# Mixture-of-experts rows written to DRAM by token and rank with indirect stores, and read back with sixteen plain loads

## The reference, cut to what matters

```python
scores = softmax(x @ w_router.T)                    # 1024 tokens x 64 experts
topw, topi = top_k(scores, 6)
combine[token, topi] = topw
routed = sum over experts e of combine[:, e:e+1] * (silu(x @ wg[e]) * (x @ wv[e])) @ wo[e]
shared = (silu(x @ swg) * (x @ swv)) @ swo
x = layernorm(x + routed + shared)                  # x: 1024 x 256, wg/wv: 64 x 256 x 176
```

## Time and profile before

| | us |
|---|---|
| median of 3 runs | 1000.24 |
| lowest, highest | 993.20, 1004.77 |
| the profiled execution | 987.55 |
| its span, first to last instruction | 985.7 |
| outside the span | 1.85 |
| mean granted TensorE clock | 0.961 |
| busy: PE, DVE, ACT, POOL | 870.2, 720.6, 510.4, 407.1 |

### The profile page before, as it was taken

How to read it: one execution, slowest core, us unless ns; L and a number is a source line. 1 busy time by engine, 2 the same in 40 slices (tenths; PEclk the granted TensorE clock), 3 DMA queues, 4 the chain that set the end, 5 groups by cost and what they waited for, 6 DMA issues and landing times.

```text
span 985.7 us, 15418 instructions
## 1 busy us (share of the span) xinstructions
PE 870.2 (88%) x5267; PEld 568.3 (58%) x5271; DVE 720.6 (73%) x1377; ACT 510.4 (52%) x1022; POOL 407.1 (41%) x338
## 2 busy tenths in 40 slices
PE   7999999999999999988889999999546867899886
PEld 3466666666565666656666777677423654343443
DVE  5667786959696867768774556665467798998797
ACT  3563554545544444445444334455522457898485
POOL 0203448494848577534214333333377312221013
PEclk9999999999999999989999999999866998999998
DMA  5451212112131221100926999999633000000001
GB/s 189 153 196 27 65 49 86 70 65 77 58 102 53 81 75 65 44 1 1 238 94 216 298 311 310 313 312 303 179 96 98 26 1 3 5 8 6 1 6 38
DMA packets 54743, 106.46 MB, mean 108 GB/s; under 512 B 8909, under 2 KB 26645, under 8 KB 54165
## 3 DMA queue, kind: packets, MB, share of 16 engines
q1 hardware_dynamic: 48917, 89.88, 29.6%
q0 software_dynamic: 5760, 15.74, 6.0%
HBM read 88.45 MB, written 17.14 MB: 107 GB/s over the span
## 4 chain that ended last, share of the span: by engine, by line
PE 54%; DVE 19%; DMA 10%; issue 5%; ACT 5%; SPq 3%; POOL 3%; DVEq 0%; ACTq 0%; POOLq 0%
PE ps L777 10%; PE ps L715 6%; DMA w_dn<-in_w_dn 5%; PE ps L873 5%; PE ps L725 4%; DVE row_max L2696 3%; PE ps L948 3%; DMA y_dram<-y_out 3%; PE ps L1280 3%; POOL key_part L1507 2%; DVE state L2119 2%; PE ps L795 2%; PE ps L960 2%; DMA key_part<-y_dram,slot_idx 2%; PE ps L1266 2%
## 5 line engine op out<-in xcount | busy, mean ns | idle before, releaser
L1479 POOL DMA_INDIRECT xg<-x_dram,tok_of x68 | 65.1, 958 | 131.8 <-PE ps L1006 94.2
L777 PE MATMUL ps<-w_vg,xT 128*128 128x512 f32 x256 | 116.8, 597 | 1.2 <-DVE th L2162 1.2
L1429 POOL TENSOR_TENSOR state<-state,rows_bc 128x1024 f32<-128x1024 f32 x22 | 53.8, 2446 | 95.5 <-DVE state L2119 41.9
L715 PE MATMUL ps<-xT,w_qks 128*128 128x512 f32 x192 | 86.5, 596 | 5.2 <-ACT qT L1585 5.2
L948 PE MATMUL ps<-w_gv,xgT 128*128 128x352 f32 (+1 forms) x272 | 87.4, 464 | 2.5 <-DMA w_dn<-in_w_dn 2.4
L2696 DVE TENSOR_REDUCE row_max<-ps 128x4 f32<-128x1024 f32 x64 | 74.3, 1217 | 7.1 <-PE ps L1245 6.3
L2130 DVE TENSOR_TENSOR aT<-ps,tri 128x768 f32<-128x768 f32 x64 | 59.7, 954 | 27.0 <-PE ps L725 26.9
L1585 ACT ACTIVATE probT<-ps 128x512 f32<-128x512 f32 x128 | 69.5, 594 | 10.1 <-PE ps L1266 9.6
L777 PEld LDWEIGHTS ps<-w_vg,xT 128*128 128x128 f32 x256 | 45.8, 190 | 48.8 <-issue 43.1
L960 PE MATMUL ps<-w_dn,hidT 88*128 88x256 f32 (+1 forms) x272 | 70.0, 379 | 0.0
L948 PEld LDWEIGHTS ps<-w_gv,xgT 128*128 128x128 f32 x272 | 48.9, 190 | 27.0 <-issue 5.2
(11 more groups left out here) (327 smaller groups left out, 2066.6 us busy)
## 6 DMA issues: line engine op xcount, KB each, us to landing
w_gv<-in_w_gv SPq DMA_DIRECT2D x68, 352.0 KB, 8.2
rows_bc<-x_dbl_dram SPq DMA_DIRECT2D x32, 512.0 KB, 3.8
w_dn<-in_w_dn SPq DMA_DIRECT2D x68, 192.0 KB, 9.6
y_dram<-y_out SPq DMA_DIRECT2D x68, 128.0 KB, 7.5
y_dram<-blank SPq DMA_DIRECT2D x4, 1408.0 KB, 13.2
w_vg<-in_wvg SPq DMA_DIRECT2D x8, 512.0 KB, 4.9
w_qks<-in_wqks SPq DMA_DIRECT2D x8, 384.0 KB, 3.1
w_o<-in_wo SPq DMA_DIRECT2D x8, 256.0 KB, 2.7
```

What stands on the lines that cost most here:

```text
L715: last = mm(bank(PJ + n % 2), w_qks[:, k, part * P:(part + 1) * P], xT[:, k, half * 512:(half + 1) * 512], start=(k == 0), stop=(k == KD - 1))
L777: last = mm(bank(PJ + t % 2), xT[:, k, t * P:(t + 1) * P], w_vg[:, k, :], start=(k == 0), stop=(k == KD - 1))
L1429: G.tensor_tensor(state_of(m), state_of(m), c_row[:, n % 2], ALU.mult).then_inc(read_out, 1)
L1479: G.indirect_dma_start(xg[:, j, :], None, x_dram, bass.IndirectOffsetOnAxis(ap=col, axis=0)).then_inc(gathered[j], 16)
```

## The change

Every row of an expert's result goes to the row of `y_dram` that belongs to its token and rank, 8 * token + rank with ranks 1 to 6 (two rows in eight stay unused). A row that belongs to no token goes to a spare row behind them. So POOL's indirect DMAs are now stores in the loop, two columns behind the gathers, and the combining reads three ranks of 128 tokens at once with a plain load on SP's queue.

- **Routing:** `scale_hot` is six ACT instructions per tile, each with the code 8 * token + rank (`tok_code`), and PE waits for each. DVE makes `tok_of` from the codes in three instructions behind one copy, drops `slot_idx`, and makes `row_of` with two more behind `groups`. Two more constants are loaded (`tok_code`, `spare`), ahead of `sh_gv` and the expert weights in SP's order.
- **Loop:** SP issues no stores. POOL, in pass i, issues for each j gather (i + 1, j), then waits for `down_copied` and issues scatter (i - 1, j). `y_out` has two halves in the fixed groups, so DVE's copy waits for the store of two groups ago. The dynamic group uses half 0 alone, waits for the scatter of the group before, and its POOL pass starts after the gathers *and* the scatters before it have landed; it copies two sets of column numbers. The last four scatters follow behind it with a third set.
- **Combining:** 16 loads of 384 KB on SP (3 KB from each of 128 token rows), four buffers, behind `f_in` and `f_out` and behind all `y_stored`.
- **Gone:** `blank`, its memset and its four stores.

```diff
-        yg = key_part[:].rearrange("p a b c -> p (a b c)").bitcast(F32).rearrange("p (n d) -> p n d", d=D)
+        yg = key_part[:].rearrange("p a b c -> p (a b c)").bitcast(F32).rearrange("p (n d) -> p n d", d=CHUNK * D)
...
-        y_out = sb("y_out", [P, NJ, D])
+        y_out = sb("y_out", [P, 2, NJ, D])
...
-            for n in range(4):
-                dst = y_dram[(E + NJ) * P + n * free:(E + NJ) * P + (n + 1) * free, :]
-                sp.dma_start(dst.rearrange("(n p) d -> p n d", p=P),
-                             blank[:].unsqueeze(1).to_broadcast([P, free // P, D])).then_inc(y_blank, 16)
...
-            def store_y(i, j):
-                sp.wait_ge(down_copied, at(i, NJ, j + 1) + TILES)
-                sp.sem_inc(load_due, 1)
-                sp.dma_start(y_dram[bass.ds(i * (NJ * P) + j * P, P), :], y_out[:, j, :]).then_inc(y_stored[j], 16)
...
             sp.wait_ge(stacked, 6)
             for dst, src in ((f_in, "f_in"), (f_out[:], "f_out")):
                 sp.dma_start(dst, a[src]).then_inc(layer_loaded, 16)
+            for j in range(NJ):
+                sp.wait_ge(y_stored[j], at(used, 16, 0))
+                sp.sem_inc(load_due, 1)
+            by_token = y_dram[0:RANKS * TOK, :].rearrange("(q e) d -> q (e d)", e=RANKS)
+            for c in range(2 * TILES):
+                if c >= 4:
+                    sp.wait_ge(combined, B + CHUNK * (c - 3))
+                first = (1 + CHUNK * (c % 2)) * D
+                sp.dma_start(yg[:, c % 4, :], by_token[c // 2 * P:(c // 2 + 1) * P, first:first + CHUNK * D]
+                             ).then_inc(back[c % 4], 16)
...
             for i in range(FIXED):
                 for j in range(NJ):
                     pool.wait_ge(xg_turned, NJ * i + j + 1)
                     gather(j, tok_of[:, NJ * (i + 1) + j:NJ * (i + 1) + j + 1])
+                    if i == 1 and j == 0:
+                        pool.wait_ge(rows_placed, 1)
+                    if i:
+                        pool.wait_ge(down_copied, NJ * (i - 1) + j + 1 + TILES)
+                        scatter(i % 2, j, row_of[:, NJ * (i - 1) + j:NJ * (i - 1) + j + 1])
             used = used_groups(pool)
             with pool.Fori(FIXED, used) as i:
                 for j in range(NJ):
                     pool.wait_ge(gathered[j], at(i, 16, 16))
-                pool.sem_inc(gather_due, 1)
+                    pool.sem_inc(gather_due, 1)
+                    pool.wait_ge(y_stored[j], at(i, 16, -16))
+                    pool.sem_inc(gather_due, 1)
                 G.tensor_copy(tok_cur[:], tok_of[:, bass.ds(i * NJ + NJ, NJ)]).then_inc(tok_picked, 1)
...
+                G.tensor_copy(row_cur[:], row_of[:, bass.ds(i * NJ - NJ, NJ)]).then_inc(row_picked, 1)
...
                     gather(j, tok_cur[:, j:j + 1])
-
+                    pool.wait_ge(down_copied, at(i, NJ, j + 1 - NJ + TILES))
+                    pool.sem_inc(gather_due, 1)
+                    scatter(0, j, row_cur[:, j:j + 1])
+            G.tensor_copy(row_last[:], row_of[:, bass.ds(used * NJ - NJ, NJ)]).then_inc(last_picked, 1)
...
             for j in range(NJ):
-                pool.wait_ge(y_stored[j], at(used, 16, 0))
-            pool.sem_inc(gather_due, 1)
-            pool.wait_ge(stacked, 6)
-            for n in range(TILES * TOPK):
-                if n >= 8:
-                    pool.wait_ge(combined, B + n - 7)
-                G.indirect_dma_start(yg[:, n % 8, :], None, y_dram,
-                                     bass.IndirectOffsetOnAxis(ap=slot_idx[:, n // TOPK, n % TOPK:n % TOPK + 1], axis=0)
-                                     ).then_inc(back[n % 8], 16)
+                pool.wait_ge(down_copied, at(used, NJ, j + 1 - NJ + TILES))
+                pool.sem_inc(gather_due, 1)
+                scatter(0, j, row_last[:, j:j + 1])
...
-                f(blk_hot[:, t % 2], blk_hot[:, t % 2], ACT.Copy, scale=tok_id[:, t:t + 1]).then_inc(hot_scaled, 1)
+                for k in range(TOPK):
+                    f(blk_hot[:, t % 2, k, :], blk_hot[:, t % 2, k, :], ACT.Copy, scale=tok_code[:, t, k:k + 1]
+                      ).then_inc(hot_scaled, 1)
...
-            V.tensor_copy(tok_of[:], ps[:, Y + 1, 0:COLS]).then_inc(route_vec, 1)
+            V.tensor_copy(code_f, ps[:, Y + 1, 0:COLS])
+            then(V.tensor_scalar(tok_f, ps[:, Y + 1, 0:COLS], -0.5 * (TOPK + 1), 1.0 / RANKS, ALU.add, ALU.mult))
+            then(V.tensor_scalar(tok_f, tok_f, ROUND, None, ALU.add))
+            V.tensor_scalar(tok_of[:], tok_f, -ROUND, None, ALU.add).then_inc(route_vec, 1)
...
-                    if not first:
+                    if half is None:
                         dve.wait_ge(y_stored[j], at(i, 16, 0))
-                    V.tensor_scalar(y_out[:, j, :], ps[:, 2 * j + 1, 256:512], 0.5, None, ALU.mult).then_inc(down_copied, 1)
+                    elif i > 1:
+                        dve.wait_ge(y_stored[j], at(i, 16, -16))
+                    V.tensor_scalar(y_out[:, half or 0, j, :], ps[:, 2 * j + 1, 256:512], 0.5, None, ALU.mult).then_inc(down_copied, 1)
```

More of the change, by code:

```diff
@@ L489, in build @@
         down_copied = sem("down_copied")
-        y_blank = sem("y_blank")
-        back = [sem(f"back{j}") for j in range(8)]
+        rows_placed = sem("rows_placed")
+        row_picked = sem("row_picked")
+        last_picked = sem("last_picked")
+        back = [sem(f"back{j}") for j in range(4)]
         combined = sem("combined")
@@ L1406, in _ @@
             nc.gpsimd.memset(x_pad[:, :, :, 0:DC - 1], 0.0).then_inc(pool_set, 1)
-            nc.gpsimd.memset(blank[:], 0.0).then_inc(pool_set, 1)
             G = nc.gpsimd
@@ L2457, in stack, with group @@
                     last.then_inc(stacked, 1)
-            def group(i, first=False, side=None):
+            def group(i, half=None, side=None):
                 for j in range(NJ):
```

73 lines of the change are left out of this document (44 added, 29 removed).

## The result

In the timing that followed the prediction the changed kernel took 1040.65 us (median of 4 runs, 1039.31 to 1043.03), the kernel before 997.98 us beside it. The ratio is 1.0425, with a 95% interval of 1.0357 to 1.0493. Forecast were 993.5 us, a range of 981 to 1010, and no measurable difference as the likeliest of the three outcomes.

The account below looks back on a forecast made before the run. Combining was POOL-bound by issuing gathers; the loop had DMA share 1.04 and PE busy 135.14 of 140 us. Terms -11.0 + 0.3 + 1.5 + 2.5 = -6.7 us, taken from 1000.24 us, gave 993.5 us, range 981 to 1010 us.

Parts of the forecast that it names:

- no measurable difference: Whole kernel: within about 1%, 10 us, of before, chance 0.46; faster 0.34, slower 0.20.
- The loop: Expert loop: stores move to POOL, eight DMAs a group, period 10.5 us instead of 10.42; +1.5 us.
- rival A: Loop becomes bound by POOL and its gathers: +19.5 or +27 us, time 1011.5 or about 1019 us; chance 0.24.
- the signs that the prediction named: Changed profile: additions from about 711 to 762 us, groups of 10.4 to 10.6 us, chunks landing in 3 to 4 us.
- Combining stage: Combining: sixteen SP loads replace 48 POOL gathers; 15.9 us of gaps go, 4.9 return as PE waits; -11.0 us.
- Routing: Routing: six ACT instructions replace one, more DVE instructions and two constants are added; +0.3 us, bounds -1.5 and +1.5.
- The formula: Loop: a group's period is 9.96 us plus half of what the gathers' landing exceeds 5.47 us.
- POOL's floor: Loop: POOL's eight DMA issues at 1.255 us each bound a group at 10.04 us.
- The gain to be set against it: Loop: the 0.68 us a group for which PE waits because of late `y_out` copies would go.
- rival B: Loop gets faster too, -4 us, and combining gains 14 instead of 11: -15 us, 985 us; chance 0.28.
- The end of the loop: Dynamic pass and last scatters: later gathers and waits for scatters make the first addition start 2.5 us later; +2.5 us.
- A rule that the forecast weighed: Loop scatters: write receipt is longest to HBM, so scatters land later than gathers and rival A is likelier; no size given.

Follow-up runs that it names:

- e11: The changed kernel, not altered, timed again beside the kernel before: 984.53 us against 987.13, ratio 0.9976.
- four later timings: The unaltered changed kernel timed on four other occasions, on chips with four different numbers: 984.53, 987.21, 986.13 and 984.78 us.
- e1: The kernel before with only the sixteen combining loads of the changed one in place of the 48 gathers: 976.94 us against 987.91, ratio 0.9887.
- e16: The changed kernel, not altered, timed again beside the kernel before: 984.78 us against 989.91, ratio 0.9977.
- e3: The changed kernel with plain stores issued by POOL, in slot order, in place of the scatters: 977.85 us, a single run.
- e4: The kernel before with a second gather behind each gather of the sixteen fixed groups, into a tile nothing reads: 1044.62 us.
- e8: The kernel before with second gathers as in e4, but two buffers for them: 1019.11 us, a single run.
- e13: The changed kernel, not altered, timed again beside the kernel before: 987.21 us against 987.73, ratio 0.9992.
- e2: The changed kernel with the scatters' row numbers in slot order, so each writes 128 neighbouring rows: 981.1 us, a single run.
- e15: The changed kernel, not altered, timed again beside the kernel before: 986.13 us against 989.18, ratio 0.9972.
- Experiment 12: The changed kernel with POOL issuing each pass's four gathers first, then its four scatters: 981.58 us, ratio to before 0.9939.
- e14: The gathers-first kernel with the wait for older stores and the row-number copy moved behind the last pass's gathers: 981.52 us against 989.18, ratio 0.9909.
- first ten experiments: Variants of the changed kernel (row numbers, layout, kind of store) and of the kernel before (new combining loads, second gathers): 976.94 to 1044.62 us.

## Why the prediction was wrong, step by step

**Against the first timing** it was wrong in its range and direction. The step that failed is "The loop": +1.5 us (with rival A's +27 at most), where +62.7 came up to the last `y_out` copy, 55 of them in the fourteen passes. Rival A was slower for another reason than its own: it asked for a POOL-bound group, with a scatter issue of 1.5 us or more or gathers that land after 7.4 us. There POOL idled 45.0 us waiting for PE, and a scatter took 1.01 us; landings can't be read in that trace. What the runs show in its place: a group of 14.9 us in which ACT takes PE's results 5.4 us after their matmuls start, against 1.5 in e11, and this in that trace alone. Its cause stays open. No row of the trace before could show it.

**Against the four later timings** the forecast of no measurable difference holds, and the gain was put too high: 0.7% forecast, 0.1 to 0.3% measured. The range of 981 to 1010 us holds all four too, but the kernel before also ran 10 to 13 us faster there than the 1000.24 that it was built on, so only the ratios count. Most of the signs that the prediction named are there in e11: groups of 10.6 us, DVE waiting for PE's projection, PE waiting for late gathers, and a scatter under 1.1 us (1.01 in the mean). The steps that failed in size are the fourteen passes, and the first pass of the loop, which had no term:

- *Combining stage, -11.0 us.* Right: 50.0 to 52.6 us in place of 61.6, so -9.0 to -11.6 (e1, with the old loop: -10.4). The mechanism too: a load landed in 3.5 us (3.1 assumed), no addition but the first waited for one in e11 (in e16 the fourth too, 1.45 us), and 4.9 us were to come back as waits for PE. In e11's waits of 700 to 770 us they are 5.1, and 6.3 to 6.7 in the other three:

```profile
DVE lk L2555 <- PE ps L1092: 5.1, 5, 2.4
```

- *Routing, +0.3 us.* Of the right size where the clock is alike: +0.5 in e11 and in e3 (39.8 against 39.3; 39.4 against e1's 38.9), 0.0 to +0.7 at a granted clock of 0.50 (43.0 against e4's 43.0 and e8's 42.3). The 43.0 us of the first timing are not the change: e4 and e8 have the old routing. What goes with them is the granted clock between 473 and 483 us, in the windows of, in this order, before, the changed kernel in the first timing, e8 and e11:

```profile
473.00:483.00 10.00, 9.29 (x54) 7.70 (x53) 5.05 (x32) 4.70 (x20) 1.77 (x8) 0.90 0.93 242
```

```profile
473.00:483.00 10.00, 10.00 (x43) 9.06 (x42) 2.12 (x8) 1.76 (x5) 1.77 (x8) 0.50 0.89 247
```

```profile
473.00:483.00 10.00, 10.00 (x43) 9.06 (x42) 2.12 (x9) 1.75 (x6) 1.76 (x8) 0.50 0.95 255
```

```profile
473.00:483.00 10.00, 8.42 (x51) 6.93 (x50) 5.19 (x33) 4.96 (x21) 1.75 (x8) 0.94 0.97 245
```

  At 0.50 the same work reaches the first gather some 3 us later (e13's 43.0 against e11's 39.8).

- *The loop, +1.5 us.* Too small: the fourteen passes take 2.8, 4.6, 5.0 and 3.9 us more in the four repeats. The formula wasn't far off: gathers land in 7.0 us in e11 (6.7 assumed), which gives T = 9.96 + 1.53 / 2 = 10.73, and a pass from 529.92 to 678.08 takes 10.58 us, where before's take 10.39 (528.07 to 673.48). What was too low is POOL's floor, 8 x 1.29 = 10.3 us and not 10.04: a scatter takes POOL 1.01 us and a gather 0.99, where 0.95 was taken for both. Nine of e11's fourteen passes lie between 10.27 and 10.40 us, at that floor; before's early ones take 9.95. So POOL has next to no slack to catch up with after a late pass. The gain to be set against it was put too high: PE's wait for DVE's hidden rows, priced at 0.68 us a group in rival B, comes 3 times for PE (1.6 us) and 6 times for its weight loads (5.0 us) in the thirteen groups of before between 560 and 700 us.

- *The first pass, no term.* It costs 1.4 to 3.7 us in the four repeats, before any scatter is issued (the first at 531.16 in e11). The first twelve matmuls of the loop, in before and in e11:

```profile
521.27 3.81 PE L948 MATMUL ps<-w_gv,xgT 128*128 128x352 f32 x12
```

```profile
521.43 5.50 PE L953 MATMUL ps<-w_gv,xgT 128*128 128x352 f32 x12
```

  The granted clock from 520 to 530 us is 1.00 in the first and 0.83 in the second. Other traces have 3.81 (e1, e2, e8) to 6.26 us (e13), and e4, the kernel before with extra gathers, 4.74, so whether the change has a part in it is open.

- *The end of the loop, +2.5 us.* Right: from the last fixed pass to the first addition the four repeats take 2.4 to 3.4 us more. The mechanism too: POOL's copy for the last pass comes 3.8 us later behind the pass before it in e11 (15.8 against 12.0), where 4.3 were forecast. In part this was luck: the last `y_out` copies wait 1.57 and 1.30 us for scatters, not 3, while PE's pauses for the gathers of group 16 and the matmuls at the lower clock (6.31 us for 3.81) had no term.

Together, from the first gather to the first addition, +7.3 us in e11 (203.3 against 196.0), +9.5 in e16, +9.9 in e15 and +11.1 in e13, where 4.0 were forecast. The stage's gain was kept, and nearly all of it was paid back ahead of it. Experiment 12 takes the passes' part away by POOL's order; e14, with the same order, has it again as waits for weights.

*A rule that the forecast weighed.* The Trainium skill (DMA: Bandwidth & Descriptors, "Anatomy of one DMA — SWDGE (gpsimd) path") has the write receipt longest where the target is HBM, so the scatters were to land later than gathers. The issues of e11 between 580 and 690 us (median landing) have them the other way round in a full queue, 6.2 against 7.0:

```profile
xg<-x_dram,tok_of POOLq DMA_INDIRECT x41, 7.0
y_dram<-y_out,row_of POOLq DMA_INDIRECT x41, 6.2
```

Nor do the last four scatters of e11 land later where the queues are nearly empty: 2.4 us (704 to 713 us), against 2.8 for the gathers of the same size in the combining stage of before. The two kinds also differ in what they read, and the receipt alone can't be seen in these rows, so they don't settle the rule itself, only that it didn't decide here.

## What to carry to other kernels

Time the unaltered changed kernel again beside the first variants: most of the first ten experiments here were aimed at a slowness that none of these chips showed, and two of its theories (P and F) needed runs of their own that one repeat would have spared. When work moves onto an engine that was half idle, price its floor per pass with the new kind of instruction in it, and put what another engine waits for (the gathers) ahead of what nobody waits for soon (the stores) in its order. A gain in a stage bound by an issuing engine is real only if the same engine doesn't become the bound of the stage that takes over its work.

## What wasn't expected of the hardware

- One program took 1040.65 us in one timing (four runs within 4 us) and 984.5 to 987.2 in four others, while the kernel before moved by 1% only. Whether that is a chip or a session, and whether it takes this kernel, is open.
- Scattered row addresses cost little: loops of 192.8 us with rows in order, 193.9 shuffled within 128 KB, 194.8 to 199.0 with a token's or a rank's layout over 6 to 16 MB, 201.5 with rows exactly 8 KB apart. Each is one trace on one chip, and repeats of one kernel spread by 3.6 us.
- A plain store of 128 KB issued by POOL takes it 0.60 us, an indirect one of the same size 1.01 us.
- In a stretch of ten microseconds (473 to 483 us) TensorE's granted clock is 0.50 in some executions of the unaltered changed kernel (the first timing, e13) and 0.84 to 0.94 in others (e11, e15, e16); the routing takes 43.0 us in the former and 39.8 to 41.2 in the latter.
